# Longer runs of one kind of matmul: attending layers in turns of four quads, the first cross-attention in turns of two key blocks

## The reference, cut to what matters

```python
# layer 0: 8 heads of 64, keys and values projected from the context and the latents
q = (l @ Wq).reshape(...); k, v = jnp.split(kv_in @ Wkv, 2, axis=-1)
out = softmax(q k^T * 64**-0.5) v           # then @ Wo

# layer 1: 16 heads of 16, a mask over the keys
out = softmax(q k^T / sqrt(16) + key_mask) (context @ wv + bv)

# layer 3: 16 heads of 16, a mask over queries and keys, keys and values are the context itself
sim = jnp.einsum('bhqd,bhkd->bhqk', q, k) / jnp.sqrt(16)
weights = jax.nn.softmax(sim + NEG_BIAS * (~mask), axis=-1)
out = jnp.einsum('bhqk,bhkd->bhqd', weights, v)
```

## Time and profile before

| | |
|---|---|
| median of 3 runs | 2570.8 us (2569.28 to 2570.88) |
| the profiled execution: its own time | 2571.34 us |
| its span | 2569.6 us |
| TensorE matmul busy | 2310.1 us (90%) |
| VectorE busy | 1831.9 us (71%) |
| ScalarE busy | 1194.1 us (46%) |
| mean granted clock of TensorE | 0.94 |

### The profile page before, as it was taken

One profiled execution on the slowest core, in us unless ns is written; L12 is line 12 of the kernel. 1 busy time (PEld: TensorE's weight loads), 2 busy tenths in 40 slices (PEclk: granted clock), 3 DMA queues, 4 the chain that ended last, 5 costly groups with the idle time before them and its releaser, 6 DMA issues. The chain is left out here.

```text
span 2569.6 us, 57124 instructions
## 1 busy us (share of the span) xinstructions
PE 2310.1 (90%) x21794; PEld 1419.9 (55%) x21794; DVE 1831.9 (71%) x2832; ACT 1194.1 (46%) x2049; POOL 520.7 (20%) x300
## 2 busy tenths in 40 slices
PE   3999989999996969999996999999997559999979
PEld 2444436666665836656665746665556415555548
DVE  6888778889886266666634388888886777777721
ACT  4566553333335337777772333333332426556552
POOL 0555440000000030000001055555662010000000
PEclk7999989999997969999997999999998669999989
DMA  8577755656645567666734422222212366676644
GB/s 275 200 245 247 264 181 143 197 164 173 183 148 189 192 160 172 161 159 162 169 79 149 163 101 100 100 100 100 79 70 53 101 131 151 158 161 152 149 139 171
DMA packets 245951, 397.62 MB, mean 155 GB/s; under 512 B 28921, under 2 KB 210304, under 8 KB 245668
## 3 DMA queue, kind: packets, MB, share of 16 engines
q1 hardware_dynamic: 240132, 393.90, 53.6%
q10 hardware_dynamic: 5664, 1.44, 0.3%
HBM read 316.44 MB, written 78.06 MB: 154 GB/s over the span
## 5 line engine op out<-in xcount | busy, mean ns | idle before, releaser
L1640 DVE CUSTOM_DVE_ANT_0 l3x_junk<-l3x_pm,l3x_mrow,l3x_top 128x896 bf16<-128x896 f32 x224 | 246.1, 1148 | 84.0 <-PE l3x_pm L1796 83.5
L1724 ACT ACTIVATE l1x_prob<-l1x_ring,mask_col 128x512 f32<-128x512 f32 x392 | 247.9, 684 | 115.9 <-PE l1x_ring L1816 114.7
L1727 ACT ACTIVATE l3x_prob<-l3x_ring 128x512 f32<-128x512 f32 x392 | 213.1, 595 | 161.1 <-PE l3x_ring L1820 161.1
L1174 ACT ACTIVATE l0x_att_pt<-l0x_att_pt 128x1024 f32<-128x1024 f32 x99 | 104.7, 1057 | 253.8 <-DVE l0x_att_pt L1109 253.8
L2804 POOL TENSOR_TENSOR l2x_gk<-l2x_f,first_vin 128x1024 f32<-128x1024 f32 x98 | 184.3, 1916 | 160.7 <-DVEq L2545 160.7
L1219 PE MATMUL l0x_att_pv<-l0x_wv,l0x_att_vin 128*128 128x512 f32 x392 | 196.0, 623 | 0.0
L2678 PE MATMUL l2x_kf<-l2w_w,l2x_nin 128*128 128x512 f32 x392 | 173.1, 601 | 4.6 <-DVE l2x_f L2519 4.5
L2678 PE MATMUL l2x_kf<-l2w_w,l2w_first 128*128 128x512 f32 x392 | 170.3, 594 | 0.0
L2519 DVE SCALAR_TENSOR_TENSOR l2x_f<-l2x_kf,l2x_rs,l2w_bias 128x1024 f32<-128x1024 f32 x98 | 125.8, 1283 | 55.3 <-PE l2x_kf L2678 43.0
L1640 DVE CUSTOM_DVE_ANT_0 l1x_junk<-l1x_pm,l1x_mrow,l1x_top 128x896 bf16<-128x896 f32 x112 | 123.7, 1148 | 56.6 <-PE l1x_pm L1796 56.6
L1640 DVE CUSTOM_DVE_ANT_0 l1x_junk<-l1x_pm,first_mrow,l1x_top 128x896 bf16<-128x896 f32 x112 | 123.4, 1147 | 49.8 <-PE l1x_pm L1796 49.8
(11 more groups left out here) (730 smaller groups left out, 4924.2 us busy)
## 6 DMA issues: line engine op xcount, KB each, us to landing
first_kt<-scratch_KS SPq DMA_DIRECT2D x84, 448.0 KB, 9.2
scratch_KT<-l0x_max_kf SPq DMA_DIRECT2D x28, 896.0 KB, 4.8
l0x_att_kt<-scratch_KT SPq DMA_DIRECT2D x56, 448.0 KB, 7.0
scratch_KS<-l0x_side_kp SPq DMA_DIRECT2D x14, 1344.0 KB, 13.5
l1x_kt<-scratch_KS SPq DMA_DIRECT2D x42, 448.0 KB, 9.6
scratch_KS<-first_kt SPq DMA_DIRECT2D x14, 1344.0 KB, 5.9
l3x_kt<-scratch_KS SPq DMA_DIRECT2D x42, 448.0 KB, 9.0
l0fw_w<-L_ffn_exp_w SPq DMA_DIRECT2D x16, 1024.0 KB, 7.7
```

The costliest lines, as they stand in the source:

```text
L1640: dve.tensor_tensor_reduce(junk[x % 2][:, :, :], pm[x % 2][:, :, 0:SPLIT], mrow[b][:, :].rearrange("p (s k) -> p s k", s=2), 1.0, top[1 - ...
L1724: ins = act.activation(into, scores, ACT.Exp, bias=R.mask_col[:, bass.ds(m * TILES + n // 4, 1)])
L1727: ins = act.activation(into, scores, ACT.Exp)
```

## The change

In the first cross-attention a turn takes two key blocks: TensorE does both blocks' `scores`, both `values`, then both `weigh` of the turn before. `l0x_att_pt` and `l0x_att_v` get four buffers each (`top_wide` moves into the fourth), VectorE does two `subtract`, two `tile`, then the two `weights_sum` of the turn before and the side work, ScalarE two exponentials and its side work; the three loops are written out in full instead of a hardware loop. In layers 1 and 3 a turn takes a key block, that is four quads: `group` of two pairs, the turn's units, both `weigh`, and in two turns of seven one more unit behind them. The quads wait for their bank one by one. There are eight `prob` buffers (`PROBS`); a unit moves to be 11 ahead; the transposition of the maxima moves from pair 6 to pair 8.

```diff
-            v = [sb(f"v{b}", [P, heads, vd]) for b in range(2)]
+            v = [sb(f"v{b}", [P, heads, vd]) for b in range(4)]
-        pt = [sb(f"pt{b}", [P, 8, P]) for b in range(2)]
+        pt = [sb(f"pt{b}", [P, 8, P]) for b in range(4)]
...
-                    after(dve, *weighed(i, t, 0))
-                    after(dve, sem(f"summed{u}"), j)
+                    if j >= 2:
+                        after(dve, sem(f"weighed{u}"), j - 1)
+                        after(dve, sem(f"summed{u}"), j - 1)
...
+                for i in range(steps):
...
+                    for t in range(0, per_body, 2):
+                        two = (t, t + 1)
+                        for n in two:
+                            subtract(i, n)
+                        for n in two:
+                            tile(i, n)
+                        for n in two:
+                            if n >= 2:
+                                weights_sum(i, n - 2)
+                            elif i:
+                                weights_sum(i - 1, per_body - 2 + n)
+                        for n in two:
+                            beside(i, n)
...
+                def begin(i, t):
+
+                    for n in (t, t + 1):
+                        scores(i, n, 0)
+                    for n in (t, t + 1):
+                        values(i, n)
...
+                for i in range(steps):
+                    for t in range(0, per_body, 2):
+                        if t + 2 < per_body:
+                            begin(i, t + 2)
+                        elif i + 1 < steps:
+                            begin(i + 1, 0)
+                        for n in (t, t + 1):
+                            weigh(i, n, 0)
...
-AHEAD_UNITS = 10
-LATE_STEPS, EARLY_STEPS = (0, 0, 2, 2, 3, 3), (5, 5, 7, 7, 9, 9, 10, 10, 12, 12)
-GAP_STEP, TOP_PAIR, SPLIT_STEP, FACTOR_PAIR = 4, 6, 7, 9
+AHEAD_UNITS = 11
+LATE_TILES, EARLY_TILES = ((0, 0), (0, 0), (0, 1), (1, 0), (1, 0)), (
+    (2, 0), (2, 0), (3, 0), (3, 0), (4, 0), (4, 0), (5, 0), (5, 0), (6, 0), (6, 0), (6, 1))
+GAP_TILE, TOP_PAIR, SPLIT_TILE, FACTOR_PAIR = 2, 8, 3, 9
+PROBS = 8
...
-                        after(pe, taken, N * (m + 1) + at - 1)
                         for n in (2 * j, 2 * j + 1):
+                            after(pe, taken, N * (m + 1) + at + n - 2 * j - 2)
                             quad(i, b, n, ring[(at + n - 2 * j) % 3]).then_inc(filled, 1)
...
-                        for j in range(PAIRS):
-                            if j + 1 < PAIRS:
-                                group(i, b, j + 1)
-                            elif exists(i, b, 1):
-                                group(i1, b1, 0)
-                            for unit in unit_list(i, b, j):
+                        for t in range(TILES):
+                            for j in (2 * t + 2, 2 * t + 3):
+                                if j < PAIRS:
+                                    group(i, b, j)
+                                elif exists(i, b, 1):
+                                    group(i1, b1, j - PAIRS)
+                            for unit in unit_list(i, b, t, 0):
                                 max_unit(*unit)
-                            weigh(i, b, j)
+                            for j in (2 * t, 2 * t + 1):
+                                weigh(i, b, j)
+                            for unit in unit_list(i, b, t, 1):
+                                max_unit(*unit)
```

More of the change, by code:

```diff
@@ L1115, in weights_sum @@
                     after(dve, sem(f"summed{1 - u}"), j + (1 if u else 0))
-                    dve.tensor_tensor(sums[:, :, :], sums[:, :, :], pt[u][:, :, :], ALU.add).then_inc(
+                    dve.tensor_tensor(sums[:, :, :], sums[:, :, :], pt[buffer(i, t)][:, :, :], ALU.add).then_inc(
                         sem(f"summed{u}"), 1)
                 def tile(i, t):
-                    b, s = t // TILES, t % TILES
                     vb, j = tile_counts(i, t)
[L1122 to L1126, removed]
@@ L1143, in _ @@
-                with dve.Fori(0, steps) as i:
-                    if project:
-                        dve.sem_inc(S.sem("values_begun"), 1)
-                        dve.tensor_copy(rs[:, :], R.rs[:, bass.ds(i * per_body, per_body)]).then_inc(sem("rs"), 1)
-                        after(dve, sem("rs"), i + 1)
[L1148 to L1151, removed]
-                        if wide and t:
-                            weights_sum(i, t - 1)
-                        s = t % TILES
-                        if s in (3, 5):
-                            side.rest_half(dve, i, t // TILES, (s - 3) // 2)
-                        if s == 5:
-                            side.low_half(dve, i, t // TILES, 0)
-                        if t == TILES:
-                            side.low_half(dve, i, 0, 1)
-                    if wide:
-                        weights_sum(i, per_body - 1)
+                    if j >= 2:
+                        after(dve, sem(f"weighed{vb}"), j - 1)
@@ L1189, in _ @@
-                act.activation(first_exp[:, :], R.ident[:, 0:1], ACT.Exp)
-                with act.Fori(0, steps) as i:
-                    for t in range(per_body):
-                        for o in range(octets):
-                            exps(i, t, o)
-                        s = t % TILES
-                        if s in (2, 4):
-                            side.high(act, i, t // TILES, s // 2 - 1)
-                        if s in (4, 6):
-                            side.middle_half(act, i, t // TILES, s // 2 - 2)
@@ L1202, in _ @@
+                exps(steps, 0)
             @block.tensor
@@ L1560, in run @@
             v = [sb(f"v{b}", [P, TILES, H, 17]) for b in range(2)]
-            pt = [sb(f"prob{u}", [P, 4, P]) for u in range(4)]
+            pt = [sb(f"prob{u}", [P, 4, P]) for u in range(PROBS)]
             junk = [sb(f"junk{n}", [P, 2, SPLIT], BF16) for n in range(2)]
```

151 lines of the change are left out of this document (71 added, 80 removed).

## The result

The changed kernel takes 2514.05 us (median of 4 runs, 2512.27 to 2516.58); the kernel before, run beside it, 2570.04 (2568.68 to 2570.88). The ratio is 0.9784, 95% interval 0.9772 to 0.9795: **faster by 56 us**. The forecast was 2520.

A forecast was written before the change was run, and what follows sets the result against it. TensorE was taken to bound all three stretches, with time lost inside its busy time. Layer 0 -25, layer 1 -8 and layer 3 -18 sum to -51 on 2571.3: 2520.3, median 0.5 lower, say 2520 us; range 2498 to 2545.

The forecast's parts named there:

- Layer 0, -25: Layer 0: halved changes of kind save 0.55 us per two blocks, -27 over 49 turns, about 2 given back: -25 us.
- The cover: Layer 0: VectorE needs 7.2 us a turn, under TensorE's 7.51, a thin margin of 0.3; if gone, the term is -12.
- The hardware loop cost nothing: Layer 0: the body of 56.42 us is 14 times 4.03, so writing the loop out saves nothing.
- Both rivals against it: Layer 0 gains 0 as loads stay uncovered (2583, chance 0.02), or doubled runs pay the change inside (2570, chance 0.03).
- rival (e): A doubled run still pays the change inside where kinds alternate in PSUM banks, other gains cancel: 2570; chance 0.03.
- Layer 1, -8: Layer 1: turn 3.73 us with a new 0.23 wait for ScalarE, chunk 28.1 against 28.69: -0.6, times 14, -8 us.
- Layer 3, -18: Layer 3: chunk 26.0 us against 27.38, -20, less 0.2 a chunk for late maxima rows, +2: -18 us.
- one of my own signs of being wrong: Chunk starts: the forecast is wrong if the first quad of a chunk waits for a transfer.
- (a): The covers fail: VectorE sets layer 0's turn (-12), ScalarE eats layer 1's gain (0), layer 3 keeps -18: 2541; chance 0.16.
- (b): Charged waits are absorbed: layer 1 gives -16, layer 3 -24, layer 0 -27: 2504; chance 0.14.
- (c): Layers 1 and 3: maxima rows late at 26 chunk boundaries, deciding from 2.0 us; at 3 us 2598, slower; chance 0.05.
- What I costed at nothing: Layers 1 and 3: eight `prob` buffers and finer bank waits add no work, only hide the exponentials' wait on the weighing.

The follow-up runs named there:

- experiment 3: Changed kernel, but layer 0 in turns of one block, the order of before, still written out with four buffers: 2543.1 us, ratio 0.9894.
- experiment 4: Changed kernel, but TensorE in layer 0 alternates values, weighing, values, weighing after two blocks of scores, two more changes of kind a turn: 2531.67 us, ratio 0.9849.
- experiment 5: Changed kernel with one more VectorE pass, a copy whose result is unused, in each turn of layer 0: 2531.93 us, ratio 0.9847.
- experiment 7: Changed kernel, but layer 1's exponentials taken of only two of a quad's four heads: 2488.09 us, ratio 0.9688.
- experiment 9: Changed kernel, but in layer 3 GpSimd copies the next chunk's values only after VectorE has copied its mask tile: 2513.02 us, ratio 0.9774.
- experiment 10: Changed kernel, but the next chunk's maxima are transposed at pair 7 instead of 8 and split in turn 2 instead of 3: 2508.86 us, ratio 0.9767.
- experiment 6: Changed kernel, but a quad of layers 1 and 3 waits for its bank together with its pair's second quad, as before: 2569.19 us, ratio 0.9996.

## Why the prediction was right, point by point

**What bounds.** Right: TensorE in all three stretches, and time hidden inside its busy time. The order alone takes 25.7 us off layer 0 at the same number of products (experiment 3).

**Layer 0, -25.** Right: -25.7, body 52.6, turn 7.51. The sizes of the changes held: 0.35 measured for the two of experiment 4, which I had at 0.36, and 0.19, 0.21 and 0.15 in the trace after for scores, values and weighing, which I had at 0.20, 0.21 and 0.15. The cover held with 0.36 us to spare (experiment 5); I had written 0.3. "The hardware loop cost nothing" is shown by experiment 3. Both rivals against it fall: by the rule of the Trainium skill on loads ("TensorE: Matmul & The Clock Gate", Part 3, The mechanism) this term would have been zero. The trace after has six steps of 0.43 in each turn's values, with a load of 0.19 under each, and disagrees. The same section also lets a load into the background weight buffer go ahead, which would fit; my reading left that out, so the zero is what one sentence of the page gives and not the whole section. That a doubled run pays inside all the same, rival (e), would have left slow products in its middle; there are none.

**Layer 1, -8.** The sign and the mechanism right, the term mis-sized: -13.1. That the turn of 3.73 was met to the hundredth, and the chunk to about 0.1, is partly luck. In the turn two steps were off against each other: the third quad came 0.10 sooner than I had it, and the fourth quad's wait is 0.32 and not 0.23 (experiment 7). In the chunk, one turn has no such wait, the two units behind the weighing cost 0.77 and 0.58 where I had 0.6 each, and maxima with factors cost 0.98 (4.39 - 3.73 + 0.32) where I had 0.8. TensorE's idle time did not "mostly go": it grew from 19.3 of 400 us to 23.9 of 380, since the new waits for ScalarE and for the late units are more than the old ones that went. What failed is "-0.6, times 14". The rescalings tell it (source view, before, then after):

```profile
L1679 DVE TENSOR_TENSOR l1x_O<-l1x_O,l1x_F x14: 692/700/700, 956.1 to 1328.8; 128x512 f32<-128x512 f32 x14
```

```profile
L1668 DVE TENSOR_TENSOR l1x_O<-l1x_O,l1x_F x14: 691/694/699, 928.8 to 1289.4; 128x512 f32<-128x512 f32 x14
```

372.7 us have become 360.6: -12. The eleven intervals in the middle give 8.0 of it, 0.73 each. The last gives 2.8 by itself (25.84 to 23.05): its chunk has five units left instead of sixteen (before the change, six), one behind a weighing instead of two, but all of the saved changes. The first gives 1.2, and 1 lies outside. A chunk that differs from the rest wants a sum of its own.

**Layer 3, -18.** Nearly right: -16.5. The sum had rounded twice: 14 x 1.38 is 19.3, not 20, and 14 x 0.2 is 2.8, not 2; unrounded its terms give -16.5, but that they meet the time is partly luck. The quickest chunk, 25.75, is better than the 26.0 of the sum. The mean, 26.12, is 0.37 above the quickest, where I had charged 0.2 for waiting: 4 us over eleven chunks. Its largest single piece, 1.6 us of waiting, was not in my sum at all: VectorE's mask copy behind GpSimd's (experiment 9). The rows of the maxima cost 0.72, 0.41 and 0.78 at three chunk ends in the changed kernel. So one of my own signs of being wrong, a first quad that waits for a transfer, was there in part: I had charged lateness, but its size, 1.9 us in the layer, is less than the 2.8 charged. Place and arrival, 10.2 and 10.1 in the forecast, were 10.15 and 10.56. The wait of 0.55 in the middle of a quad (at 2371.8) names no releaser in the profile and is open.

**The rivals.** (a) did not come: both covers held. (b) did not come either: the waits that I charged were not absorbed, and TensorE's idle time grew in both layers (19.3 to 23.9 us, and 13.7 of 380 to 18.3 of 358). That layer 1 gained 13.1, nearer to its 16 than to my 8, has the causes given above. (c), rows too late by over 2.0 us a chunk, did not come. It needs no slower VectorE, though, only keys still in flight, as experiment 10 shows with 6 to 7 us for a transfer of about 2; the longest wait of a first quad in layer 3 in any run is 1.84 us, at the last chunk end of experiment 3, where the first transfer took 6.4.

**What I costed at nothing.** The waits a bank at a time were described as adding no work and hiding a wait. In the new order they are worth 55 us (experiment 6), nearly twice what the two layers gain together, 29.6.

## What to carry to other kernels

Inside a fully busy TensorE, compare a run's first product with its last, and the step into the next kind with the step inside the run; the difference (here 0.15 to 0.21 us) times the number of changes is what longer runs can give. Before lengthening a run, ask what it makes wait: the banks must be waited for one by one, and the engine that empties them needs its own timetable. Where a wait remains, put a piece of another kind into it: there its change of kind is nearly free (0.10 us for a unit and two changes).

## What the runs showed of the hardware that I had not expected

A bfloat16 copy of 128x896 on VectorE takes 0.38 us, and 1.76 to 1.79 when a GpSimd copy of 1.68 us has started just before it; with GpSimd made to wait, 13 of 13 take at most 0.384. Both are copies from and to SBUF. The Trainium skill, "SBUF — State Buffer", section "SBUF: two separate sides", says that VectorE in one of its two-port modes and GpSimd take a shared pair of ports as an exclusive lock, and the one that comes second is blocked for the whole instruction. The trace agrees: from 2149.99 GpSimd's copy had 1.53 us to go, and VectorE's took 1.79; that rest and its own 0.38 would be 1.91, so the copy lasts as if it had waited for nearly all of it. No view shows whether this copy runs in a two-port mode. Such an encounter depends on when a transfer lands, so it comes in one chunk and not the next; the kernel before had one copy of 1.48 among fourteen.

In layer 3 the small transfer of the rows took 5.8 to 7.4 us from issue to landing with large ones before it on the same queue still under way, and 1.4 to 3.0 where those had landed or nearly so. The Trainium skill, "DMA: Bandwidth & Descriptors", section "Two DMAs through the same engine are not ordered", says that descriptors of one queue start in order on an engine. The trace fits, but does not exclude that the engines' share alone does it. The consequence is shown: issuing earlier does not mean landing earlier.
